# Context handed over with its features on the partitions, four chunk buffers, and a shorter order of the first batch

## What is computed

```
xn   = layernorm(x)
Q    = (xn Wq + bq), 16 heads of 32;   K = ctx Wk + bk,  V = ctx Wv + bv   (one K and one V of 32 columns for all heads)
x1   = x + softmax(Q K^T / sqrt(32)) V Wo + bo
x2   = x1 + memory(layernorm(x1))      (a gated delta rule, 4 heads of 128, chunks of 64: a triangular inverse per head)
out  = x2 + expert(layernorm(x2))      (top 1 of 16 experts, relu, capacity 128 rows each)
```

## Time and profile before

| | |
|---|---|
| Median of 3 runs | 2176.65 us (2176.55 to 2177.91) |
| Span of the profiled execution | 2171.3 us |
| Median minus that span | 5.35 us |
| Busy: PE, POOL, DVE, ACT | 97%, 75%, 59%, 56% of the span |
| Busy before 1705 us (the attention part, and its end): PE, POOL | 1640, 1397 us |
| DMA | 262 MB, mean 121 GB/s |

### The profile page before, as it was taken

How to read it: one execution, slowest core, us unless ns; L and a number is a source line. 1 busy time by engine, 2 the same in 40 slices (tenths; PEclk the granted TensorE clock), 3 DMA queues, 4 the chain that set the end, 5 groups by cost and what they waited for, 6 DMA issues and landing times. The chain is left out here.

```text
span 2171.3 us, 35745 instructions
## 1 busy us (share of the span) xinstructions
PE 2095.7 (97%) x12908; PEld 1421.6 (65%) x12908; DVE 1272.3 (59%) x2226; ACT 1220.7 (56%) x2277; POOL 1635.7 (75%) x1387
## 2 busy tenths in 40 slices
PE   7879999999999999999999999999989999999999
PEld 5436565656565656666565656565645789999998
DVE  5656767676666666676767676766664433333332
ACT  3756575666666566666665666666655233433333
POOL 0778888888888888888888888889798145555555
PEclk8989999999999999999999999999999999999999
DMA  4752121212212121212131212112200089999994
GB/s 159 242 113 90 48 74 45 73 52 66 75 48 74 45 73 53 74 44 82 39 97 43 74 43 74 59 57 71 79 15 11 12 313 357 363 352 359 360 348 177
DMA packets 107055, 262.31 MB, mean 121 GB/s; under 512 B 8960, under 2 KB 34304, under 8 KB 98688
## 3 DMA queue, kind: packets, MB, share of 16 engines
q1 hardware_dynamic: 96912, 234.92, 31.6%
q10 hardware_dynamic: 6384, 14.62, 2.3%
q0 software_dynamic: 3584, 10.49, 1.2%
HBM read 223.67 MB, written 25.72 MB: 115 GB/s over the span
## 5 line engine op out<-in xcount | busy, mean ns | idle before, releaser
L1094 POOL TENSOR_TENSOR psum<-psum,weights 128x512 f32<-128x512 f32 x896 | 1152.6, 1286 | 163.4 <-ACT weights L702 60.5
L880 DVE TENSOR_REDUCE mpart<-bank 128x1 f32<-128x512 f32 x1024 | 680.4, 684 | 308.9 <-PE bank L447 300.0
L702 ACT ACTIVATE weights<-bank 128x512 f32<-128x512 f32 x1024 | 597.0, 599 | 324.1 <-PE bank L460 313.3
L460 PE MATMUL bank<-qT,kT 97*128 97x512 f32 x1024 | 482.8, 477 | 10.0 <-DMA qT<-mrow 6.5
L447 PE MATMUL bank<-kT,qT 96*128 96x512 f32 x1024 | 450.0, 451 | 9.6 <-DVE mpart L880 6.8
L447 PEld LDWEIGHTS bank<-kT,qT 96*128 96x128 f32 x1024 | 196.9, 192 | 141.2 <-issue 87.4
L1346 POOL TENSOR_TENSOR w2l<-w,w2h 128x1024 fp32r<-128x1024 f32 x64 | 202.9, 3171 | 75.8 <-PE ebank L1259 54.5
L460 PEld LDWEIGHTS bank<-qT,kT 97*128 97x128 f32 x1024 | 195.7, 193 | 89.4 <-issue 49.2
L472 PE MATMUL bank<-weights,v 128*32 128x512 f32 x2048 | 251.3, 609 | 0.0
L737 ACT COPY w_first<-bank 128x512 f32<-128x512 f32 x248 | 144.7, 584 | 67.6 <-PE bank L412 64.6
L1289 ACT ACTIVATE hh<-ebank 128x512 fp32r<-128x512 f32 x64 | 38.2, 597 | 224.6 <-PE ebank L1243 224.6
(11 more groups left out here) (174 smaller groups left out, 3019.3 us busy)
## 6 DMA issues: line engine op xcount, KB each, us to landing
w<-in_w SPq DMA_DIRECT2D x48, 2048.0 KB, 19.9
w_first<-in_ctx SPq DMA_DIRECT2D x62, 1024.0 KB, 5.2
w_first<-in_w SPq DMA_DIRECT2D x16, 2048.0 KB, 12.2
dispatched<-route ACTq DMA_DIRECT2D x17, 513.0 KB, 8.5
dis<-dispatched SPq DMA_DIRECT2D x16, 513.0 KB, 3.5
qT<-qh SPq DMA_DIRECT2D x128, 64.0 KB, 3.4
qT<-qs SPq DMA_DIRECT2D x64, 64.0 KB, 2.1
xr<-in_x SPq DMA_DIRECT2D x16, 256.0 KB, 2.7
```

Source lines behind the costliest of these rows:

```text
L460: e.matmul(B_BANK[u % 2][:], kT[b % 2][0:3 * HD + 1, k * P:(k + 1) * P], qT[b % 2][0:3 * HD + 1, g * 512:(g + 1) * 512], start=True, stop= ...
L702: e.activation(p[n % NP], B_BANK[u % 2][:], ACT.Exp).then_inc(p_act.sem, 1)
L880: e.tensor_reduce(mpart[g % 2][:, 4 * (n % 4) + n // 4:4 * (n % 4) + n // 4 + 1], max_bank(b, g, n)[:], AX.X, ALU.max).then_inc(max_dve.se ...
L1094: e.tensor_tensor(acc[:], first, p[(UNITS * b + u) % NP], ALU.add).then_inc(psum_pool.sem, 1)
```

## The change

1. The host lays the context out as `(batch, chunk, feature in the plane, plane, row)`: a chunk now arrives with features on the partitions, as `cxT` wants it. The transposes (L526), the copies (L737, L905) and their semaphores and bank turns are gone; `wkv` multiplies the loaded chunk itself. A chunk is 512 consecutive context rows now; it was every fourth group of four.
2. `w1_first` holds four chunk buffers. A chunk's buffer is reloaded for the next batch four ticks after its `kv` products, which SP waits for: ticks 22, 41, 62 and 78.
3. `FIRST` is shorter: `kv` at 7, 10, 16, 18, query projection at 11 to 14, the first group's maxima at 24 to 31 (all after the last `kv`), their turn at 33. The first batch's 4 dummy matmuls come at tick 10.
4. The host lays out Wq, Wo, WwT, WrT and Wg by planes, so that a partition's part is one contiguous piece.

Ticks and places of everything else stay. The core of the diff:

```diff
-WARM = {-1: 14, 14: 4}
+WARM = {-1: 14, 10: 4}
...
-STEADY = Prep(norm=-32, xn=-29, xnt=-27, qproj=[24, 26, 27, 29], qsend=52,
-              tiles=[9, 12, 13, 15, 18, 24, 27, 32, 35, 39, 44, 50, 53, 54, 60, 69],
-              kv=[18, 37, 58, 74], vt=[42, 79])
+STEADY = Prep(norm=-32, xn=-29, xnt=-27, qproj=[24, 26, 27, 29], qsend=52, kv=[18, 37, 58, 74], vt=[42, 79])
...
-FIRST = Prep(norm=6, xn=9, xnt=12, qproj=[14, 15, 16, 17], qsend=22,
-             tiles=[2, 3, 4, 5, 6, 7, 8, 9, 19, 20, 21, 22, 28, 29, 30, 31], kv=[10, 23, 33, 38], vt=[27, 43])
-LOAD_AT = [13, 45, 71, 80]
+FIRST = Prep(norm=4, xn=6, xnt=8, qproj=[11, 12, 13, 14], qsend=19, kv=[7, 10, 16, 18], vt=[20, 22])
+LOAD_AFTER, W1_AT = 4, 80
...
-FIRST_MAX, FIRST_TURN = [35, 35, 36, 36, 40, 40, 41, 41, 42, 42, 43, 43, 44, 44, 45, 45], 47
+FIRST_MAX, FIRST_TURN = [24 + n // 2 for n in range(KB)], 33
...
-        cx = [w1_first[:, c, :].rearrange("p (k d) -> p k d", k=4) for c in range(2)]
-        cxT = [w1_first[:, 2 + c, :].rearrange("p (c t) -> p c t", c=DC) for c in range(2)]
+        cxT = [w1_first[:, c, :].rearrange("p (c t) -> p c t", c=DC) for c in range(4)]
...
             def load_ctx(b, c):
-                if b and c >= 2:
-                    e.wait_ge(*t_pe.at(b, 4 * c - 5))
-                elif b > 1:
-                    e.wait_ge(*t_pe.at(b - 1, 4 * c + 11))
-                elif b:
-                    e.wait_ge(*t_pe.at(0, 4 * c + 3))
-                e.dma_start(chunk(b, c), T["ctx"][b].rearrange("(p c k) d -> c p k d", c=4, k=4)[c]).then_inc(
-                    ctx_in[c].sem, 16)
+                if b:
+                    e.wait_ge(*kv_pe.at(b - 1, c))
+                e.dma_start(cxT[c], T["ctx"][b, c]).then_inc(ctx_in[c].sem, 16)
...
-                    if t in LOAD_AT and i >= -1:
-                        c = LOAD_AT.index(t) + 2
-                        if 0 < i + 1 + c // 4 < B:
-                            load_ctx(i + 1 + c // 4, c % 4)
+                    if 0 <= i + 1 < B - 1 and t - LOAD_AFTER in prep(i + 1).kv:
+                        load_ctx(i + 2, prep(i + 1).kv.index(t - LOAD_AFTER))
...
-                    transposes(turn_bank(b, ("t", k)), lambda j: chunk(b, c)[:, kk, j * P:(j + 1) * P]).then_inc(t_pe.sem, 1)
...
                     c = prep(b).kv.index(t)
-                    e.wait_ge(*copied(b, 4 * c + 3))
+                    e.wait_ge(*ctx_in[c].at(b))
...
-                        ins = e.matmul(KV_BANK[rows, :], wkv[:, j, :], cxT[c % 2][:, j, :], start=j < 2, stop=j >= 2)
+                        ins = e.matmul(KV_BANK[rows, :], wkv[:, j, :], cxT[c][:, j, :], start=j < 2, stop=j >= 2)
...
-                    e.copy(cxT[c % 2][:, :, kk * P:(kk + 1) * P],
-                           turn_bank(b, ("t", k))[:].rearrange("p (c t) -> p c t", c=DC)).then_inc(cxT_act.sem, 1)
...
-                    e.tensor_copy(cxT[c % 2][:, :, kk * P:(kk + 1) * P],
-                                  turn_bank(b, ("t", k))[:].rearrange("p (c t) -> p c t", c=DC)).then_inc(cxT_dve.sem, 1)
...
+    ctx = np.ascontiguousarray(g["ctx_1024"].reshape(B, 4, S // 4, DC, P).transpose(0, 1, 4, 3, 2))
```

More of the change, by code:

```diff
@@ L237, in level @@
             return (b, lv) if b < LAST else (b, 4 * lv + part)
-        uses = sorted((TICKS * b + t, b, use) for b in range(B) for t, use in
-                      [(prep(b).xnt, ("x", 0))] + [(t, ("t", k)) for k, t in enumerate(prep(b).tiles)]
-                      + [(t, ("v", c)) for c, t in enumerate(prep(b).vt)])
-        turns, holds, first_uses = {}, {}, 0
-        for _, b, use in uses:
-            place = 0
-            if b == 0:
-                place, first_uses = first_uses % 4, first_uses + 1
-            turns[b, use] = place, holds.get(place)
-            holds[place] = b, use
-        def copied(b, k):
-            if b:
-                return cxT_act.at(b, k - KB // 2)
-            return cxT_dve.at(0, k // 2) if k % 2 else cxT_act.at(0, k // 2)
-        def turn_bank(b, use):
-            return [T_BANK, *B_BANK, PV_BANK][turns[b, use][0]]
+        turns = [(b, use) for _, b, use in sorted(
+            [(TICKS * b + prep(b).xnt, b, ("x", 0)) for b in range(B)]
+            + [(TICKS * b + t, b, ("v", m)) for b in range(B) for m, t in enumerate(prep(b).vt)])]
         def turn_read(b, use):
-            if turns[b, use][1] is None:
-                return None
-            before_b, (kind, i) = turns[b, use][1]
-            if kind == "x":
-                return xnT_act.at(before_b)
-            return copied(before_b, i) if kind == "t" else v_act.at(before_b, i)
+            n = turns.index((b, use))
+            if n == 0:
+                return None
+            before_b, (kind, m) = turns[n - 1]
+            return xnT_act.at(before_b) if kind == "x" else v_act.at(before_b, m)
         kv_uses = [(b, use) for _, b, use in sorted(
@@ L327, in weight @@
         def weight(e, dst, src):
-            return e.dma_start(dst, T[src].rearrange("(c p) n -> p c n", p=P))
+            return e.dma_start(dst, T[src])
         @block.sync
@@ L392, in _ @@
                             e.dma_start(T["out"][b], x2).then_inc(x2_out.sem, 16)
-                    if t == LOAD_AT[3] and i == LAST - 1:
+                    if t == W1_AT and i == LAST - 1:
                         e.wait_ge(*kv_pe.at(LAST, 3))
@@ L724, in prepare @@
                     e.wait_ge(*xnT_pe.at(b))
-                    e.copy(xnT[:].rearrange("p c t -> p (c t)"), turn_bank(b, ("x", 0))[:]).then_inc(xnT_act.sem, 1)
+                    e.copy(xnT[:].rearrange("p c t -> p (c t)"), T_BANK[:]).then_inc(xnT_act.sem, 1)
                 if t == prep(b).qproj[3] + 2:
@@ L730, in prepare @@
                     e.copy(qh[:], qs[:]).then_inc(q_act.sem, 1)
-                if t in prep(b).tiles and (b or prep(b).tiles.index(t) % 2 == 0):
-                    k = prep(b).tiles.index(t)
-                    c, kk = divmod(k, 4)
-                    e.wait_ge(*t_pe.at(b, k))
-                    if kk == 0 and (b or c >= 2):
-                        e.wait_ge(*(kv_pe.at(b, c - 2) if c >= 2 else kv_pe.at(b - 1, c + 2)))
-                    e.copy(cxT[c % 2][:, :, kk * P:(kk + 1) * P],
-                           turn_bank(b, ("t", k))[:].rearrange("p (c t) -> p c t", c=DC)).then_inc(cxT_act.sem, 1)
                 if t in prep(b).kv:
```

42 lines of the change are left out of this document (12 added, 30 removed).

## The result

| | before | after |
|---|---|---|
| median of the runs, us | 2177.28 (2176.55 to 2178.03, 4 runs) | 2140.73 (2138.95 to 2144.96, 4 runs) |
| ratio | | 0.9836, 95% interval 0.9824 to 0.9849 |
| profiled execution: time, span | | 2144.96, 2143.16 |
| granted clock over the span | | 0.982 |
| first exponential | 50.40 | 50.83 |

The account below looks back on a forecast made before the run. POOL was taken to bound half of each steady period, with PE's full list beside it, and the inverse's chains through PE, DVE and ACT the other. Gains 45 + 3.6 + 7 = 55.6 us gave 2121 us, range 2090 to 2160.

Parts of the forecast that it names:

- Tick 98 to `rk`: Half of a steady period limited by POOL: POOL's wait goes (0.8 us) and ACT's slack behind `rn` (0.6), 1.4 us.
- `rk` to the inverse: Steady period: ACT's copy of the tile at 39 goes, 0.6 us; PE's tile at 44 before the keys' product, 0.4.
- Level 0: In the inverse, per steady period: tile at 50 hid in a wait, 0; those at 53 and 54 gain 0.5 us.
- Level 1: In the inverse: ACT's key cast no longer stands behind the copy of tile 60, 0.4 us; tile at 69 gives 0.
- Steady sum: Gain per steady period: terms add to 3.3 us, taken as 3.2; over 14 periods 45 us (11 to 97).
- The start: Before the first period: query projection 0.6 us sooner, first group's maxima 3.0 less, together 3.6 us (-1 to 5).
- The first period: From 49.7 to 149.3 us: eight tiles about 5 us, free DMA time 2, together 7 us (3 to 10).
- New waits and moved DMAs: nothing: Waits for reloaded chunks, and query and maxima transfers near the moved loads, were claimed to cost 0 us.
- the rival that ended slower: PE's waits lower its granted clock to 0.91 in every period, of 108.5 us then; time 2252 us, chance 0.05.
- The forecast's own span: Total time 2092 to 2148 us, from 2 to 5 us per period and 7 to 14 for the rest; chance 0.65.
- POOL gives way: PE runs further ahead of POOL, all tiles count in steady periods: 14 x 6.9 = 97 us, time 2069; chance 0.13.
- The chains hold: Second half of each period gains nothing, ACT is held before `rk`: 14 x 0.8 = 11 us, time 2159; chance 0.17.

## Why the prediction was right, and where it was not

The forecast was 2121 us with 2090 to 2160 around it, and faster at 0.93; the time is 2140.7. The direction and the mechanism held; the gain is two thirds of what I summed. From the second batch's first exponential to the end of the last one's the profiles gained 32.7 us, the first period 3 and the start nothing: 36 of the 36.5. Step by step:

- **Tick 98 to `rk`** (1.4): right. The addition to `rk` takes 50.9 us, POOL's wait for the mean is gone, its eight additions start 1.42 us apart as before (850.11, 11.22 us for eight), and ACT waits 1.09 us for `rn`. `rk` begins 0.03 us after `rn` has ended, where I had allowed 0.1.
- **`rk` to the inverse** (0.6 + 0.4): 0.64. This term was the first to be too large. From `rk` to the copy `V` it was 3.53 us before and is 3.08 now, 0.45 instead of 0.6, and up to the product of the keys 0.76 (5.80 and 5.04), so the tile at 44 gave 0.3. The last 0.1 went in PE's own list between that product and the turn of `XT1`. POOL, which was late at `XT1`, wasn't the reason, as the run with three additions on DVE shows.
- **Level 0** (0.5): 0.2. The first product of level 1 begins 7.68 us behind the copy `xn` where it was 7.90; that is the tile at 54. The one at 53 gave nothing: DVE had a maximum and the reduction to `mneg` ahead of the subtraction, which begins 3.91 us behind `xn` in the kernel before and 3.92 after.
- **Level 1** (0.4): 0.1; with level 0 it is 0.36 where I had 0.9. The copy of the tile at 60 is gone, and ACT's key cast begins 0.69 us sooner than before, counted from `xn`, but DVE's next instruction takes 0.35 longer (see the last section), and level 1's subtraction comes 0.36 sooner.
- **Steady sum**: 2.35 instead of 3.2, 0.85 in each of 14 periods: 12 of the 19 us that are missing. The two sets of tiles put back separately (1.93 where the terms gave 2.4, 0.37 where they gave 0.9) agree with this; of the early ones the tile at 18 was put back at 19.
- **The start** (3.6): nothing. The 3.0 for the maxima in one run was 2.7. The 0.6 for the query projection was wrong in sign: it came 2.4 us later in the profile. I had seen the `kv` group in front of it and not that both write the same bank, nor what the low clock makes of the group. The range of -1 to 5 holds it.
- **The first period** (7): 3 on average. The 5 for the tiles is about right, 4.3 without a backlog by one pair of executions. The 2 for free DMA time had the wrong sign: with the backlog PE waits about 10 us for maxima transfers, where it waited 6. I had priced the moved load and the later queries at nothing because of ticks in hand; the transfer that mattered was the small one behind them. What exactly makes two waits out of one is open: moving the load back didn't do it.
- **"New waits and moved DMAs: nothing"** held for the steady periods, where PE waits for no transfer. There the kernel's DMA share is 0.22.
- **Steady clock**: 1.00, as forecast, so the rival that ended slower had no ground. (Its 108.5 should read 108.3, from 103.3 and 5.)
- **The forecast's own span**: 2 us per period and 7 for the rest are 35 us, so its upper end is 2142 and not 2148. The measured 2140.7 lies just inside.

Of the rivals, "POOL gives way" is refuted by the period. "The chains hold" was nearer to the truth than its chance of 0.17 said: the whole time, 2140.7, is as far from its 2159 as from the forecast's 2121, though the steady period of 100.05 is nearer to the forecast's 99.2 than to its 101.6. Behind `rk` half of the gain is lost (1.0 instead of 1.9), to PE's own list, to DVE's list and to steps that were priced too high. And the Trainium skill's rule, Perfetto Trace Analysis, section Identifying the Most-Contended Engine, by which I gave POOL at 87.5 of 102.4 room and called PE the bound, I had applied in part only. The same section of the Trainium skill says that matmul busy time is no good measure for TensorE, and to take the share of peak FLOPs and the busy time of its weight loads instead. These were busy 62.17 of 102.4 us, less than POOL, so by their busy time POOL was the engine to improve, and the 97 us didn't follow from it. The result lies between: the tiles gave 2.35 of the 6.9 us, and three additions less on POOL gave 0.43 more.

## What to carry to other kernels

A gain on a chain is worth its size only up to the next instruction that waits for something else. Follow each term to the first instruction whose start doesn't move, and stop counting there. An engine that starts late isn't yet the one that holds the chain: look whether the next step waits for it (here PE didn't). Price a small transfer by what stands in the queues ahead of it, not by the ticks in hand, and profile a stretch with a backlog twice before you explain its waits: one execution here was 10 us off.
